# Layer-1 experts: queries and keys of two experts from seven block products in place of eight, with two of three operand sums on POOL

## What is computed

```python
rw = _gating(hidden_states, sim_matrix, gates).reshape(b, t, E)
q = jnp.einsum('btc,ech,bte->bth', hidden_states, q_proj, rw)
k = jnp.einsum('btc,ech,bte->bth', hidden_states, k_proj, rw)
v = jnp.einsum('btc,ech,bte->bth', hidden_states, v_proj, rw)
scores = jnp.einsum('bqh,bkh->bqk', q, k) * scale
attn = jax.nn.softmax(jnp.where(causal[None], scores, -jnp.inf), axis=-1)
ao = jnp.einsum('bqk,bkh->bqh', attn, v)
out = jnp.einsum('bth,ehc,bte->btc', ao, o_proj, rw)
```

## Time and profile before

| | us |
|---|---|
| median of 3 executions | 3118.76 |
| lowest and highest | 3117.68, 3125.38 |
| the profiled execution | 3116.84 |
| its span in the trace | 3115.3 |
| the stage (SP's first load to the next stage's first load) | 734.2 to 1742.6 |

### The profile page before, as it was taken

The page is one execution under the profiler, slowest core; times in us unless marked ns, Lnnn a source line. Parts: engine busy times, 40 slices in busy tenths (PEclk is TensorE's granted clock), DMA queues, the critical chain, the costliest instruction groups (busy, mean ns, idle before and its releaser), DMA issues. The chain is left out here.

```text
span 3115.3 us, 66235 instructions
## 1 busy us (share of the span) xinstructions
PE 2616.4 (84%) x24651; PEld 1742.5 (56%) x24686; DVE 2055.4 (66%) x5077; ACT 1340.4 (43%) x2225; POOL 396.7 (13%) x558
## 2 busy tenths in 40 slices
PE   4867669995999999999999698987979776887457
PEld 3734446664656665665665466664657554666327
DVE  6789869995354545545454388897840386888784
ACT  3558868882010000001000377764534344666364
POOL 0012210000000000000000000001321341323104
PEclk9988779997999999999999799998989898989778
DMA  3110000002131122113111000001013220000001
GB/s 92 30 66 1 0 23 15 13 10 109 55 99 65 55 76 88 54 55 103 59 54 55 19 13 15 13 2 32 27 33 100 83 69 6 0 0 0 8 0 54
DMA packets 55136, 128.71 MB, mean 41 GB/s; under 512 B 9669, under 2 KB 21317, under 8 KB 53962
## 3 DMA queue, kind: packets, MB, share of 16 engines
q1 hardware_dynamic: 47466, 106.36, 10.4%
q0 software_dynamic: 7520, 20.34, 2.2%
HBM read 109.37 MB, written 17.30 MB: 41 GB/s over the span
## 5 line engine op out<-in xcount | busy, mean ns | idle before, releaser
L1435 PE MATMUL banks<-l1f_xe,l1f_w 128*128 128x512 f32 x1024 | 486.2, 597 | 7.9 <-DVE l1f_xe L1630 7.9
L1630 DVE TENSOR_TENSOR l1f_xe<-l1f_hT,l1f_rwb 128x512 f32<-128x512 f32 x256 | 173.4, 692 | 315.9 <-PE banks L1437 307.9
L1437 PEld LDWEIGHTS banks<-l1f_w,l1f_xe 128*128 128x128 f32 x2048 | 269.2, 192 | 123.2 <-issue 123.2
L1437 PE MATMUL banks<-l1f_w,l1f_xe 128*128 128x128 f32 x2048 | 269.8, 275 | 0.0
L1435 PEld LDWEIGHTS banks<-l1f_xe,l1f_w 128*128 128x128 f32 x1024 | 177.0, 192 | 138.4 <-issue 130.2
L1636 DVE TENSOR_TENSOR l1f_ae<-l1f_aoT,l1f_rwb 128x512 f32<-128x512 f32 x256 | 161.5, 685 | 128.6 <-PE banks L1465 128.6
L1465 PE MATMUL banks<-l1f_ae,l1f_w 128*128 128x512 f32 x512 | 233.9, 596 | 7.1 <-DVE l1f_ae L1636 7.1
L1465 PEld LDWEIGHTS banks<-l1f_ae,l1f_w 128*128 128x128 f32 x512 | 91.2, 190 | 106.0 <-issue 66.4
L214 POOL COPY x<-xn 128x512 f32 (+1 forms) x16 | 9.8, 611 | 966.2 <-DVE xn L1660 966.2
L1517 ACT ACTIVATE l1f_gw<-l1f_gw 128x64 f32<-128x64 f32 x16 | 4.1, 256 | 272.6 <-DVE l1f_gw L1611 272.6
L1105 DVE TENSOR_REDUCE l2a_top<-banks 128x16 f32<-128x1024 f32 x64 | 78.3, 1223 | 34.6 <-PE banks L1052 33.7
(11 more groups left out here) (499 smaller groups left out, 6124.4 us busy)
## 6 DMA issues: line engine op xcount, KB each, us to landing
l1f_rwb<-l1f_shares SPq DMA_DIRECT2D x128, 512.0 KB, 4.8
l0a_ctxT<-in_ctxT SPq DMA_DIRECT2D x16, 256.0 KB, 2.6
l2f_sent<-l0f_zero SPq DMA_DIRECT2D x4, 1024.0 KB, 7.0
l1a_ctxT<-in_ctxT SPq DMA_DIRECT2D x16, 256.0 KB, 2.6
l2c_ctxT<-in_ctxT SPq DMA_DIRECT2D x16, 256.0 KB, 2.6
l2e_rows<-l2f_sent SPq DMA_DIRECT2D x16, 256.0 KB, 2.8
l2f_answers<-l2e_y POOLq DMA_DIRECT2D x16, 256.0 KB, 2.7
l3p_ctxT<-in_ctxT SPq DMA_DIRECT2D x16, 256.0 KB, 2.6
```

What stands on the lines that cost most here:

```text
L1435: pe.matmul(bank, w[:, n, e, :], xe[:, e % NB, :], start=(e == 0), stop=(e == E - 1))
L1437: last = pe.matmul(v_bank[:, D * j:D * j + D], xe[:, e % NB, P * j:P * j + P], w[:, 2, e, :], start=(e == 0 and j == 0), stop=(e == E - 1) ...
L1630: dve.tensor_tensor(xe[:, e % NB, :], hT[:, m, :], rwb[:, m, e, :], ALU.mult).then_inc(s.xe_ready, 1)
```

## The change

- Queries and keys: two experts (a pair, e1 = 2p and e2 = 2p + 1) and the two halves of the group's tokens (`HT` = 256) form a 2x2 by 2x2 block product, q and k of both halves from both experts. It was eight block products of 256 columns (done as four of 512); it is now seven products M1 to M7 of 256 columns, in four banks (`prods`), summed over the eight pairs. Their moving operands are the weighted halves (`own_parts`: minus first half for e1, second half for e2; `cross_parts`: second half for e1, first half for e2) and four sums of them (`sums`, ring of 2): `first_sums` makes two on DVE in one instruction of 512 elements, `second_sum` and `third_sum` make one each on POOL, of 256 elements. Their stationary operands are plain and combined weights (`mixes`, made once by `mix` on DVE and `minus` on ACT). After the last pair DVE joins the seven products to q and k (`join`, four instructions).
- Values: same count and size of products. The first half comes from the negated weights `wv_minus` where the operand is negated.
- `xe` and `ae` share one ring `feed` of NB = 8.
- `norm` goes to ACT (four activations); `copy_hT` is three copies of 256 columns, one negated.
- `score`, `turn_p`, `weigh`, `centre`, `exp`, `normalise` move from group n - 1 in the second half of the step to group n - 2 in the first half. ACT now does the subtraction of the maximum, the sum and the scaling of the softmax (four exponentials and four copies of 128 columns).
- `turn_rw` moves from before expert 14 of the first half to behind the first output product. `turn_y` moves before output product 3, `new_x` before `weigh_ao` 10.
- POOL's copy of x (`xb_pool`) goes; `k.xb` holds v and yT.

Core of the diff:

```diff
-            def qkv(g, e):
-                pe.wait_ge(s.xe_ready, E * g + e + 1)
...
+            def qkv(g, p):
+                at, sm = 2 * p % NB, p % RING_S
+                e1, e2 = 2 * p, 2 * p + 1
+                pe.wait_ge(s.parts_ready, 2 * (PAIRS * g + p + 1))
...
+                product(M1, mixes[:, W1_MINUS, p, :], feed[:, at, 0:HT], p, True)
+                product(M4, mixes[:, T4_MINUS, p, :], feed[:, at, HT:GT], p, True)
+                for j in range(TG):
+                    first, c = j < TG // 2, P * j
+                    pe.matmul(v_bank[:, D * j:D * j + D], feed[:, at, c:c + P], wv_minus[:, p, :] if first else w[:, 0, e2, :],
+                              start=(p == 0 and j == 0), stop=False, skip_group_check=True)
+                for j in range(TG):
+                    first, c = j < TG // 2, (P * j + HT) % GT
+                    pe.matmul(v_bank[:, D * j:D * j + D], feed[:, at + 1, c:c + P], w[:, 0, e2 if first else e1, :],
+                              start=False, stop=(p == PAIRS - 1), skip_group_check=True)
+                product(M2, wq[:, p, :], feed[:, at + 1, HT:GT], p, True)
+                pe.wait_ge(s.first_ready, PAIRS * g + p + 1)
+                product(M7, mixes[:, T3_MINUS, p, :], sums[:, sm, 0, :], p, True)
+                product(M5, mixes[:, T1, p, :], sums[:, sm, 1, :], p)
+                pe.wait_ge(s.second_ready, PAIRS * g + p + 1)
+                product(M6, mixes[:, T2, p, :], sums[:, sm, 2, :], p)
+                pe.wait_ge(s.sums_ready, PAIRS * g + p + 1)
+                product(M3, wk[:, p, :], sums[:, sm, 3, :], p).then_inc(s.qkv_psum, 1)
...
+            def second_sum(g, p):
+                at, sm = 2 * p % NB, p % RING_S
+                pool.wait_ge(s.first_ready, PAIRS * g + p + 1)
+                settle(pool, k)
+                pool.tensor_tensor(sums[:, sm, 2, :], sums[:, sm, 1, :], feed[:, at, 0:HT], ALU.add).then_inc(s.second_ready, 1)
+
+            def third_sum(g, p):
...
+                pool.tensor_tensor(sums[:, sm, 3, :], feed[:, at + 1, HT:GT], sums[:, sm, 2, :], ALU.subtract).then_inc(s.sums_ready, 1)
...
+            def first_sums(g, p):
+
+                at, sm = 2 * p % NB, p % RING_S
+                dve.wait_ge(s.parts_ready, 2 * (PAIRS * g + p + 1))
+                wait(dve, s.qkv_psum, PAIRS * g + p - RING_S + 1)
...
+                dve.tensor_tensor(sums[:, sm, 0:2, :], two(feed[:, at, :]), two(feed[:, at + 1, :])[:, 0:1, :].to_broadcast([P, 2, HT]),
+                                  ALU.add).then_inc(s.first_ready, 1)
```

More of the change, by code:

```diff
@@ new lines, in product @@
+            def product(n, left, right, p, first=False):
+                return pe.matmul(prods[:, n, :], left, right, start=(p == 0 and first), stop=(p == PAIRS - 1), skip_group_check=True)
+            def qkv(g, p):
+                at, sm = 2 * p % NB, p % RING_S
+                e1, e2 = 2 * p, 2 * p + 1
+                pe.wait_ge(s.parts_ready, 2 * (PAIRS * g + p + 1))
+                if p == 0:
+                    pe.wait_ge(s.weights, 16 * 2)
+                    pe.wait_ge(s.mixes_ready, 1)
+                    pe.wait_ge(s.wv_minus_ready, 1)
+                    wait(pe, s.q_joined, g)
@@ L1568, in _ @@
             finish_stats_dve(dve, k, s)
-            chain = Chain(dve, s.w_chain)
+            start = chain = Chain(dve, s.w_chain)
             dve.wait_ge(s.gate_weights, 16 * 2)
@@ L1662, in new_x @@
-                x_update_dve(dve, k, s, g, m, add)
+                wait(dve, s.x_done, g - 1)
+                dve.tensor_tensor(k.xn[:, m], k.x[:, bass.ds(TG * g, TG), :], att_bank.rearrange("p (t c) -> p t c", c=D), ALU.add)\
+                    .then_inc(s.xn_ready, 1)
+                dve.wait_ge(s.xn_ready, g + 1)
+                stats_of_xn(dve, k, s, g, m, TG)
             def step(n, m, live):
                 chain = Chain(dve, s.g_chain, n, 24)
-                for e in range(E):
+                if isinstance(n, int) and n == 1:
+                    mix(start)
@@ L1667, in step @@
+                for p in range(PAIRS):
                     if live(1):
[L1668 to L1674 removed]
+                        if p > 0:
+                            first_sums(n - 1, p - 1)
+                        own_parts(n - 1, m(1), p)
+                        cross_parts(n - 1, m(1), p)
+                    if p == 2 and live(2):
+                        centre(n - 2)
+                    if p == 4 and live(2):
+                        normalise(n - 2)
+                    if 3 <= p <= 7 and live(0):
+                        gate(n, chain, p - 3)
@@ L1675, in step @@
+                if live(1):
+                    first_sums(n - 1, PAIRS - 1)
+                if live(0):
+                    gate(n, chain, 5)
                 for e in range(E):
                     if e == 6 and live(1):
-                        centre(n - 1)
-                    if e == 9 and live(1):
-                        normalise(n - 1)
+                        join(n - 1)
+                    if e == 10 and live(3):
+                        new_x(n - 3, m(3))
                     if live(2):
```

278 lines of the change are left out of this document (179 added, 99 removed).

## The result

The changed kernel takes **3096.59 us** (median of 4 runs, 3093.96 to 3097.56); the kernel before took 3122.07 on the same chip. The ratio is 0.9929, 95% interval 0.9913 to 0.9946: faster, by 0.5 to 0.9%, some 22 us. The forecast was 49 us, and 3096.59 lies above its range of 3062 to 3092.

What follows compares the result with a forecast made beforehand. PE's instruction stream was taken to bound the kernel; seven terms summed to -49.2 us, from 3116.84 to 3067.6, and with 1.9 for the median the forecast was 3069 us, range 3062 to 3092 for 8 in 10.

Steps and rivals of the forecast that it cites:

- term 2: Full steps: PE's 0.65 us of idle time a step goes in 14 steps, -9.1 us, with DVE's work ready in time.
- Term 1: q and k of a pair on PE: 14 x 0.216 us replace 8 x 0.429, 0.41 less, -52.1 us in all.
- the rule on half-width products: Skill's spacings for PE: 256 columns cost 0.75 of 512, making the change +134 us, about 3255; the prediction went against it.
- Term 3: First half, per pair: POOL's sums about 0.7 us each, hidden by 5 us or more; DVE's work 36 us of 56.4.
- Term 4: Three more waits a pair on PE: 0.1 us a step, +1.6 us; upper end +73.
- rival B: PE's waits before M7, M6 and M3 expose weight loads: slower, 3140 us; chance 0.05 together with the half-width cost.
- Term 5: Stage's start: norm on ACT, hT in three copies and PE waiting for both parts, +1.5 us.
- Term 6: Groups 0 to 1: 11.4 us of waiting and lower clock in place of 9.2 idle or slow, +2.2 us.
- Term 7: The tail, with group 15's softmax uncovered on PE: 41.6 us in place of 34.9, +6.7 us.
- Rival A: DVE and POOL block each other and PE waits: 1 to 2 us a step, 3083 to 3097 us; chance 0.14.
- The sign that was to show A: PE idle time named after `l1f_sums` or `l1f_feed` in the trace; no size given.
- a step above 58: Listed sign that the forecast is wrong: a step above 58 us, where 56.4 to 57 was expected in the middle.

Runs made afterwards that it cites:

- pad4: Changed kernel with 4 instructions that do nothing put ahead of the layer-1 loop in DVE's stream: 3067.30 us, ratio 0.9844 to the kernel before.
- pool_twice: Changed kernel with 4 idle DVE instructions ahead of the loop, plus one more 256-column sum on POOL in each pair: 3064.82 us.
- alldve: Changed kernel with second and third sums made by DVE, none by POOL, and 51 idle DVE instructions ahead of the loop: 3061.03 us.
- pad128: Changed kernel with 128 idle DVE instructions ahead of the layer-1 loop and 128 behind it: 3118.74 us.
- behind4: Changed kernel with one more round written out ahead of the layer-1 loop, no padding: 3069.76 us.

## Why the prediction was wrong, and where it was right

**The step that failed** is in term 2: "the next step's first two parts are ready at 12.7, wanted at 14.3." It counts DVE's instructions by their durations and takes it that they are there to be run. The lead is nearly right (1.6 forecast, 2.1 measured), but in four of the steps DVE stopped for 8.20, 7.68, 7.97 and 7.69 us before it, because the instructions had to be fetched. Less 2.1 each that is 23.1 us, just what PE waited, and PE's lower clock behind each wait gives the rest of the 32.9. No term, no bound and no rival had the length or the place of DVE's loop in it, although the program has both: 286 long before, 302 after, and pushed 51 places on by the new instructions ahead of it, from place 76 of a page to place 127, its last (counted from 0, with the border where the stops put it). Pad4 moves it four places further on, and nothing is fetched.

Without that, point by point, against pad4's trace:

- *The stage as a whole*: forecast -49.2 us; measured 1008.4 to 957.9, **-50.5**. The forecast time was 3069, pad4's median is 3067.3, taken with another group of runs of before (3117.05).
- *Term 1*, 0.41 us a pair, -52.1: the eighth product put back costs 56.5 (0.44 a pair; 16 MATMULs of 256 take 3.46 where 8 of 512 took 3.43). Right. The weight against the rule on half-width products was right too: products of 256 stay at 0.216.
- *Term 2*, no idle time left in a full step: PE busy 56.47 of 56.52, right, apart from the four jumps.
- *Term 3*: POOL's sums were put at 0.7 us and measured 0.97 and 0.88, inside the bounds, and hidden as forecast. What the term left out is what the exclusion does to DVE: its second product takes 1.15 us in place of 0.68, and its work in a step is 41 us and not 36.
- *Term 4*, waits in front of M7, M6 and M3: 56.52 against 56.46, right; rival B is out.
- *Term 5*, the first product 1.5 us later: 26.4 us after the stage's start in place of 25.2, 1.2.
- *Term 6*: PE's idle time before group 1's first product is 9.05 us (about 10 forecast), with the lower clock behind it:

```profile
813.55 2.08 PE L1469 MATMUL banks<-l1f_feed,l1f_mixes 128*128 128x256 f32 x4 [9.05 <-DVE l1f_feed L1752]
```

- *Term 7*, the tail: from the first output product behind the last pair (1647.84) to the end of group 15's output (1688.13) 40.3 us; 41.6 forecast, 34.9 before. The parts (pad4):

```profile
1662.23 1.05 PE L1506 MATMUL banks<-l1f_qk 128*128 128x128 f32 x8
1667.33 0.66 PE L223 MATMUL banks<-consts,l1f_prob 128*128 128x128 f32 x4 [4.04 <-ACT l1f_prob L1613]
1668.65 2.07 PE L1519 MATMUL banks<-l1f_h,xb 128*128 128x128 f32 x8 [0.67 <-ACT l1f_h L1618]
1672.13 4.40 PE L1526 MATMUL banks<-l1f_feed,l1f_w 128*128 128x512 f32 x6 [1.40 <-DVE l1f_feed L1785]
```

- *Rival A*: the exclusion is real and costs DVE 5.9 us a step, and PE nothing; pool_twice and alldve exclude it as a cause. The result of 3096.59 lies within A's times (3083 to 3097), and one who read only the median would have taken A for shown.
- *The sign that was to show A*, "PE idle named after `l1f_feed`", did appear, and so did "a step above 58", with another cause. What parted them was that 31.5 us of DVE's idle time stood under "issue", in front of one line, four times.

What stays open: the unchanged stages behind this one took between 1363.9 us (alldve) and 1376.8 (pad128) in the traces (1372.7 before, 1366.7 in the changed kernel, 1369.2 in pad4), with no common cause found. Of the 19.3 us between the two profiled runs the stage gives 16.9; the stages ahead of it took 3.6 more and those behind it 6.0 less. So medians that differ by some us, as those of pad4, alldve and behind4, say nothing of the stage by themselves.

## What to carry to other kernels

Before costing an edit to a loop, count all the instructions of each engine's loop, waits and register work too, and see where the loop begins: here one that needed a fourth page of 128 lost up to 9 us at each jump, and a handful of idle instructions or one more round ahead of it took that back. A gap at each second step, or whatever the loop's round is, with DVE idle under "issue" (or under a releaser that was long done) and instruction packets beside it, points to this fault; here moving the loop cured it with the work untouched. And price help from POOL by what it does to DVE's own instructions: here they grew by 5.9 us a step for the 6.8 that it took over.
